# Layer 0's pairs in six tiles of 128 rows and one tile that holds the 34 left three times

## The reference

```python
e = stack([tbl_f[ids[:, f]] for f in range(39)], axis=1)        # (2048, 39, 16)
x0, xk = e, e
for idx, (W, b) in enumerate([(w0, b0), (w1, b1), (w2, b2)]):   # 128 outputs each
    z = relu(einsum('bhd,bkd,hks->bsd', x0, xk, W) + b)
    if idx != 2:
        xk = z[:, :64]
        direct.append(z[:, 64:])
    else:
        direct.append(z)
z = sum(concatenate(direct, axis=1), axis=-1)                   # (2048, 256)
h = concatenate([z, dense_ctx], axis=1)
h = relu(h @ W_top1 + b_top1); h = relu(h @ W_top2 + b_top2)
y = h @ W_top3
```

## Time and profile before

| | |
|---|---|
| time, median of 3 runs | 2412.33 us (2410.93 to 2412.48) |
| the profiled execution | 2410.21 us, span 2408.4 us |
| TensorE busy | 2343.9 us, 97% |
| VectorE busy | 2253.5 us, 94% |
| GpSimd busy | 2001.8 us, 83% |
| ScalarE busy | 1305.4 us, 54% |
| moved by DMA | 475.43 MB, mean 197 GB/s |
| granted TensorE clock, mean | 0.996 of full |

### The profile page before, as it was taken

The page is one execution under the profiler, slowest core; times in us unless marked ns, Lnnn a source line. Parts: engine busy times, 40 slices in busy tenths (PEclk is TensorE's granted clock), DMA queues, the critical chain, the costliest instruction groups (busy, mean ns, idle before and its releaser), DMA issues.

```text
span 2408.4 us, 32379 instructions
## 1 busy us (share of the span) xinstructions
PE 2343.9 (97%) x7936; PEld 1499.0 (62%) x7936; DVE 2253.5 (94%) x2241; ACT 1305.4 (54%) x1534; POOL 2001.8 (83%) x1284
## 2 busy tenths in 40 slices
PE   2899999999999999999999999999999999999999
PEld 1566666666666666666666666666666666666655
DVE  3799999999999999999999999999999999999973
ACT  2455555555555555555555555555555555555542
POOL 5888898898888889889888888988888888898630
PEclk9999999999999999999999999999999999999999
DMA  7977887787787788778778778877877887887610
GB/s 196 229 189 201 220 214 186 211 232 179 207 229 199 193 217 213 187 211 235 178 207 226 199 194 217 225 179 211 231 182 203 226 204 191 214 225 182 197 57 1
DMA packets 403715, 475.43 MB, mean 197 GB/s; under 512 B 171409, under 2 KB 180625, under 8 KB 403425
## 3 DMA queue, kind: packets, MB, share of 16 engines
q1 hardware_dynamic: 304055, 310.13, 52.8%
q10 hardware_dynamic: 79163, 159.95, 21.6%
q0 software_dynamic: 20480, 5.15, 1.8%
HBM read 465.41 MB, written 9.71 MB: 197 GB/s over the span
## 4 chain that ended last, share of the span: by engine, by line
PE 95%; POOL 2%; DMA 2%; issue 1%; SPq 0%; ACT 0%; DVE 0%; ACTq 0%; POOLq 0%
PE z L718 92%; POOL rows L515 1%; DMA xb<-x_rows 1%; POOL low L546 1%; DMA rows<-table,index 0%; PE x L813 0%; PE z L832 0%; PE prod_dve L813 0%; PE z L834 0%; PE z L791 0%; PE z L837 0%; SPq L426 0%; DMA x_rows<-rows 0%; PE x L814 0%; PE x L815 0%
## 5 line engine op out<-in xcount | busy, mean ns | idle before, releaser
L546 POOL TENSOR_TENSOR low<-prod_pool,high 128x1024 fp32r<-128x1024 f32 (+1 forms) x576 | 1379.4, 2395 | 206.8 <-ACT high L886 200.1
L718 PE MATMUL z<-prod_whole,w_whole 128*128 128x512 f32 (+2 forms) x2432 | 1130.5, 594 | 42.2 <-DVE prod_whole L601 42.2
L718 PE MATMUL z<-high,w_high 128*128 128x512 f32 (+1 forms) x1792 | 864.4, 482 | 17.9 <-ACT high L886 13.7
L886 ACT ACTIVATE high<-prod_pool 128x1024 fp32r<-128x1024 f32 (+1 forms) x576 | 611.0, 1061 | 407.5 <-DVE prod_pool L601 234.5
L718 PEld LDWEIGHTS z<-prod_whole,w_whole 128*128 128x128 f32 (+2 forms) x2432 | 461.8, 190 | 426.9 <-issue 365.6
L718 PE MATMUL z<-high,w_low 128*128 128x512 f32 (+1 forms) x1792 | 708.4, 395 | 0.0
L515 POOL DMA_INDIRECT rows<-table,index x640 | 611.1, 955 | 116.0 <-issue 102.2
L601 DVE TENSOR_TENSOR prod_pool<-xh,x 128x1024 f32<-128x1024 f32 x512 | 622.8, 1216 | 36.4 <-ACT x L864 33.3
L601 DVE TENSOR_TENSOR prod_whole<-xh,x 128x1024 f32<-128x1024 f32 (+1 forms) x576 | 615.6, 1096 | 6.1
L886 ACT ACTIVATE high<-prod_dve 128x1024 fp32r<-128x1024 f32 (+2 forms) x384 | 338.8, 882 | 481.6 <-DVE prod_dve L601 319.3
L718 PE MATMUL z<-low,w_high 128*128 128x512 f32 (+1 forms) x1664 | 554.4, 427 | 0.6 <-POOL low L546 0.6
(11 more groups left out here) (59 smaller groups left out, 405.2 us busy)
## 6 DMA issues: line engine op xcount, KB each, us to landing
xh<-x_rows SPq DMA_DIRECT2D x63, 2560.0 KB, 17.7
xh<-x_rows ACTq DMA_DIRECT2D x63, 2432.0 KB, 19.2
xb<-x_rows SPq DMA_DIRECT2D x128, 546.0 KB
xb<-x_rows SPq DMA_DIRECT2D x63, 468.0 KB
xa<-x_rows SPq DMA_DIRECT2D x191, 78.0 KB
rows<-table,index POOLq DMA_INDIRECT x640
xh<-x_rows SPq DMA_DIRECT2D x65, 128.0 KB, 20.5
x_rows<-rows SPq DMA_DIRECT2D x256, 20.0 KB
```

Of the source, the lines that this page charges most:

```text
L546: pool.tensor_tensor(low[0:g.rows, g.split_slot, 0:n, :], prod_pool[0:g.rows, g.slot, 0:n, :], high[0:g.rows, g.split_slot, 0:n, :].bitcas ...
L718: return pe.matmul(z[stage][:, :], weights[0:g.rows, table[stage, g.tiles[i]], :], src[0:g.rows, i, :], start=g.begins_layer and first, st ...
L886: act.activation(high[0:g.rows, g.split_slot, 0:n, :], src[0:g.rows, 0:n, :], ACT.Copy).then_inc(high_ready, 1)
```

## The change

Layer 0 gets six tiles of 128 rows: 117 as before (REST = 6 tiles of three shifts) and eleven rows of a further shift, 18 + tile (`MORE`, `MORE_AT`). Of the 780 pairs 34 are left. The seventh tile, number 6, holds 40 rows with these pairs three times, at rows 0, 40 and 80. VectorE multiplies it (from `xa_rest`), ScalarE rounds all of it, VectorE overwrites the first 40 rows with the low parts, and the weights are laid out so that rows 0 to 79 have w_high and rows 80 to 119 w_low. One rounded pass (`rest_pass`) then does what three do elsewhere. Tiles 0 and 1 become WHOLE, tile 6 BY_DVE; there is no BY_DVE pair in layer 0 any more.

The loads of pairs per chunk grow from six DMAs to twenty: two for the eleven rows (22 KB and 132 KB), and four for each copy of the 40 rows, each of ten outer rows by two, 40 KB. The rows of the low parts' copy are the first. The unused rows are cleared once. The MLP's second context input moves to a product slot, as there are 27 instead of 28 split weight tiles.

```diff
-T0 = -(-SHIFTS // JT)
-LAST0 = (SHIFTS - JT * (T0 - 1)) * F
+T0 = SHIFTS // JT + 1
+REST = T0 - 1
+MORE = 128 - JT * F
+MORE_AT = JT * REST
+LEFT, LEFT_AT, LEFT_RUN, LEFT_STEP = 40, 10, 10, 19
+FOR_HIGH_W, FOR_LOW_W = (0, LEFT), (2 * LEFT,)
...
-    0: [(WHOLE, 6, 1), (BY_DVE, 0, 2), (BY_POOL, 2, 2), (WHOLE, 4, 2)],
+    0: [(WHOLE, 0, 2), (BY_DVE, REST, 1), (BY_POOL, 2, 2), (WHOLE, 4, 2)],
...
+X0_LOADS = 2 * JT + 2 + 12
...
-                    "ctx": [w[0:CTX, CTX_AT:CTX_AT + MB], w[0:CTX, CTX_AT + MB:CTX_AT + 2 * MB]],
+                    "ctx": [w[0:CTX, CTX_AT:CTX_AT + MB], x[0:CTX, 4 + n1, :]],
...
-        def load_pairs(engine, c, shifts):
+        def load_pairs(engine, c, shifts, rest):
             of = rows_of(c)
+            step = of.ap[0][0]
             for jj in shifts:
-                n = (SHIFTS - jj + JT - 1) // JT
                 at = slice(jj * F, (jj + 1) * F)
                 engine.dma_start(xa[at, :], of[0:F, :]).then_inc(x0_loaded, 16)
-                step = of.ap[0][0]
                 shifted = bass.AP(tensor=of.tensor, offset=of.offset + jj * step,
-                                  ap=[[step, F], [JT * step, n], [1, CN]])
-                engine.dma_start(xb[at, 0:n, :], shifted).then_inc(x0_loaded, 16)
+                                  ap=[[step, F], [JT * step, REST], [1, CN]])
+                engine.dma_start(xb[at, 0:REST, :], shifted).then_inc(x0_loaded, 16)
+            if not rest:
+                return
+            engine.dma_start(xa[JT * F:128, :], of[0:MORE, :]).then_inc(x0_loaded, 16)
+            shifted = bass.AP(tensor=of.tensor, offset=of.offset + MORE_AT * step,
+                              ap=[[step, MORE], [step, REST], [1, CN]])
+            engine.dma_start(xb[JT * F:128, 0:REST, :], shifted).then_inc(x0_loaded, 16)
+            for at in FOR_HIGH_W + FOR_LOW_W:
+                for s in range(2):
+                    half = slice(at + s * LEFT // 2, at + (s + 1) * LEFT // 2)
+                    for rows, field in ((xa_rest, LEFT_AT + s), (xb[:, REST, :], LEFT_AT + LEFT_STEP)):
+                        runs = bass.AP(tensor=of.tensor, offset=of.offset + field * step,
+                                       ap=[[step, LEFT_RUN], [LEFT_STEP * step, 2], [1, CN]])
+                        engine.dma_start(rows[half, :], runs).then_inc(x0_loaded, 16)
...
+                else:
+                    sp.wait_ge(rest_cleared, 2)
-                load_pairs(sp, c, range(2 if c.known and c.n == 0 else JT))
+                load_pairs(sp, c, range(2 if c.known and c.n == 0 else JT), True)
...
-                part = slice(H, 128) if g.half else slice(0, g.rows)
-                into = (high if g.half else low)[part, g.split_slot, 0:n, :]
+                part = slice(H, 128) if g.half else slice(0, LEFT) if g.rest else slice(0, g.rows)
+                into = (high if g.stacked else low)[part, g.split_slot, 0:n, :]
...
+                    other = xa_rest if g.rest else shared
...
+            dve.memset(xa_rest[:, :], 0.0).then_inc(rest_cleared, 1)
+            dve.memset(xb[:, REST, :], 0.0).then_inc(rest_cleared, 1)
...
+                    if g.rest:
+                        dve.tensor_tensor(w_low[:, to, :], stage_sb[:, T0:T0 + 1, :],
+                                          w_low[:, to, :].bitcast(f32), ALU.subtract).then_inc(w_ready, 1)
+                        dve.wait_ge(w_ready, ready - 1)
+                        dve.tensor_tensor(w_high[:, to, :], w_high[:, to, :].bitcast(f32),
+                                          w_low[:, to, :].bitcast(f32), ALU.add).then_inc(w_ready, 1)
+                        continue
...
+                def rest_pass(g):
+                    wait_count(pe, low_by_dve, c, g, g.of_kind + 1, BY_DVE)
+                    mm(g, w_high, SPLIT_TILE, high[:, g.split_slot, :, :], 0, True, True
+                       ).then_inc(products_used, 1)
...
-                act.activation(xa_ps[0:JT * F, :], xa[:, :], ACT.Copy).then_inc(xa_copied, 1)
+                act.activation(xa_ps[:, :], xa[:, :], ACT.Copy).then_inc(xa_copied, 1)
...
-            load_pairs(act, Chunk(0, 0), range(2, JT))
+            load_pairs(act, Chunk(0, 0), range(2, JT), False)
```

More of the change, by code:

```diff
@@ L107, in __init__ @@
         self.half = stage > 0 and first == HALF_TILE
-        self.rows = 128 if stage else (LAST0 if first == T0 - 1 else JT * F)
+        self.rest = stage == 0 and first == REST
+        self.rows = 128
+        self.stacked = self.half or self.rest
         self.split = self.kind != WHOLE
@@ L131, in in_order_of_use @@
     for g in groups:
-        late = g.split and not g.half
-        if behind and (late or g.half or g.ends_layer):
+        late = g.split and not g.stacked
+        if behind and (late or g.stacked or g.ends_layer):
             yield behind
@@ L665, in _ @@
                     to, src = weight_tiles(g)
+                    dve.wait_ge(w_rounded, sum(1 + before.rest for before in firsts[:i + 1]))
+                    ready += 1 + g.half + g.rest
+                    if g.rest:
[5 more added lines that the diff above has]
+                        continue
                     part = slice(0, H) if g.half else slice(0, 128)
-                    dve.wait_ge(w_rounded, i + 1)
                     dve.tensor_tensor(w_low[part, to, :], src[part], w_high[part, to, :].bitcast(f32),
@@ L762, in contract @@
                         half_passes(g)
+                    elif g.rest:
+                        rest_pass(g)
                     elif g.ends_layer:
@@ L772, in chunk @@
                 contract(2, c)
-            pe.wait_ge(w_ready, sum(g.split for g in PLAN[0, 0]))
-            pe.wait_ge(w_rounded, len(GROUPS[0]))
+            pe.wait_ge(w_ready, sum(g.split + g.rest for g in PLAN[0, 0]))
+            pe.wait_ge(w_rounded, sum(1 + g.rest for g in PLAN[0, 0]))
             contract(0, Chunk(0, 0))
             pe.wait_ge(w_ready, W_READY)
-            pe.wait_ge(w_rounded, N_GROUPS)
+            pe.wait_ge(w_rounded, N_ROUNDED)
             over_chunks(pe, chunk)
@@ L1002, with place @@
     w0 = a["L0_rec_w0"]
-    w0a = np.zeros((128, T0, S), w0.dtype)
-    w0b = np.zeros((128, T0, S), w0.dtype)
-    first = np.arange(F)
-    for j in range(SHIFTS):
-        second = (first + j) % F
-        at = slice(j % JT * F, (j % JT + 1) * F)
-        w0a[at, j // JT] = w0[first, second]
-        if j:
-            w0b[at, j // JT] = w0[second, first]
+    w0a = np.zeros((128, STAGED0, S), w0.dtype)
+    w0b = np.zeros((128, STAGED0, S), w0.dtype)
+    placed = set()
+    def place(f, g, at, tile):
+        if f != g:
+            w0b[at, tile] = w0[g, f]
+        w0a[at, tile] = w0[f, g]
+        placed.add(frozenset((f, g)))
+    for tile in range(REST):
+        for jj in range(JT):
+            for f in range(F):
+                place(f, (f + JT * tile + jj) % F, jj * F + f, tile)
+    for tile in range(REST):
+        for f in range(MORE):
+            second = (f + MORE_AT + tile) % F
+            if frozenset((f, second)) not in placed:
+                place(f, second, JT * F + f, tile)
+    left = []
+    for r in range(LEFT):
+        s, k, run = np.unravel_index(r, (2, LEFT_RUN, 2))
+        f = int(LEFT_AT + s + LEFT_STEP * run + k)
+        pair = (f % F, int(LEFT_AT + LEFT_STEP * (run + 1) + k) % F)
+        if frozenset(pair) not in placed:
+            placed.add(frozenset(pair))
+            left.append((r, pair))
+    for tile, copies in ((REST, FOR_HIGH_W), (T0, FOR_LOW_W)):
+        for r, pair in left:
+            for at in copies:
+                place(*pair, at + r, tile)
+    assert len(placed) == F * (F + 1) // 2
     def by_fields(w):
```

39 lines of the change are left out of this document (23 added, 16 removed).

## The result

| | before | after |
|---|---|---|
| median | 2411.63 us (4 runs, 2410.14 to 2412.48) | 3018.15 us (4 runs, 3013.23 to 3022.27) |
| ratio | 1 | 1.252, interval 1.2503 to 1.2537 |
| a chunk, from the first last relu to the last one | 35.30 us | 44.56 us |

A forecast was written before the change was run, and what follows sets the result against it. TensorE's own pace was taken to bound the kernel after the start, at 35.37 us a chunk. 2410.2 - 18.6 + 7.5 = 2399.1, and 2.1 more for a median: 2401 us, range 2394 to 2410.

The forecast's parts named there:

- TensorE 0.30 us less a chunk: TensorE's layer 0: 5.36 us becomes 5.06 a chunk; over 62 chunks 18.6 us less.
- VectorE makes one single and three pair products as before: VectorE's layer 0: products unchanged, low part 0.53 us less, so about 34.3 of 35.07 us busy.
- 14 more issues, 0.5 us apart: SyncE's loads of pairs, twenty instead of six a chunk: 6.9 us more issuing, hidden by its other waits.
- the third rival: Pairs come too late in every chunk at ScalarE's copy of xa: slower, 2513 us with copies 0.8 us each; chance 0.15.
- 24 packets x 0.148 = 3.6 us: Steady-state pair loads: the added 0.49 MB, cut in ten outer rows on ten engines, lands 3.6 us later.
- up to 7: Steady-state pair loads: delay in us of the added bytes if they take turns with ScalarE's xh stream.
- I take 4: Steady-state pair loads: chosen delay 4 us, landing at about 1027 against a limit of about 1030.6; steady state pays nothing.
- xh comes 4 us later, 10 us before it is wanted: The xh load in the steady state: 4 us later behind the added pairs, still 10 us early.
- the second leg: From the copy of xa to the next first load of pairs; 15.8 us would have been left for it.
- Everything behind 74.8 moves by: Start: 3 us for chunk 0's loads plus 4.5 for chunk 1's pairs, together 7.5 us, bounds 3.6 and 11.7.
- the ring: Copy of xa, then VectorE's layer 0 and sums, which release the next stores and loads; bites beyond 7.8 us later landing.
- the first leg: From the first load of pairs to the copy of xa; the prediction allowed 19.6 us (1010.96 to 1030.6).

The follow-up runs named there:

- free copies: Changed kernel with the copies loaded in chunk 0 only and xa_rest copied to PSUM by ScalarE before VectorE multiplies: 2399.13 us.
- the kernel before with twelve loads: Kernel before, plus twelve 40 KB loads into a buffer nobody reads, which the copy of xa waits for: 2887.39 us.
- the run with twenty rows: Changed kernel, each load of copies taking twenty consecutive rows instead of ten rows by two (wrong pairs): 2798.79 us.

## Why the prediction was wrong

- *TensorE 0.30 us less a chunk*: right. 35.05 us with free copies.
- *VectorE makes one single and three pair products as before*: wrong for the single one, which took 0.68 us before. The nearest row had one factor in PSUM; here both are in SBUF, 1.1 us on average in the changed kernel and 2.06 where GpSimd is busy. With the copies loaded once the kernel took 2426.7 us with this product and 2399.1 with one factor in PSUM.
- *14 more issues, 0.5 us apart*: mis-sized. The twelve copies cost 0.88 each (10.6 us); more than the 0.8 of the third rival.
- *"24 packets x 0.148 = 3.6 us", "up to 7", "I take 4"*: this step failed, and it decides. Landing moved from the 11.8 us reckoned to over 24, not to 16. The pairs were through 12.5 us after their first issue, nearly as reckoned; the 240 rows of the copies took 12.2 us more, not 4. With ScalarE's xh kept away they took 5.4, so the 3.6 was not far off for a queue by itself. What was mis-sized is the term "taking turns with ScalarE's xh stream it is up to 7", which was priced by counting queues. That the copies suffer from this stream is shown by moving it (24.75 to 17.3 us). Why so much is argued only: the copies' last rows (80 to 119) and ScalarE's xh (64 to 127) lie in one half, and in 1024 to 1029 the two queues share 207 GB/s, of which the copies' queue gets 0.19 of 1.03 MB. That a shared half has this effect is shown for xh against xh alone, and few engines for a load stay a rival.
- *xh comes 4 us later, 10 us before it is wanted*: wrong in kind. Not only its start moved. The halves of xh fell out of step and ran at 207 to 209 GB/s for much of their time instead of 398, and 17.7 us to landing became 27.2. SyncE's half then lay in its queue before the stored rows, whose issue took 4.5 us in the mean instead of 3.0 (5.83 in the period shown): most of what the second leg grew by.
- *"Everything behind 74.8 moves by" 7.5 us*: mis-sized in both of its terms. Copies of `xa` for chunk 1, before, in the changed kernel and in the one with copies in chunk 0 alone and `xa_rest` in PSUM:

```profile
74.79 0.60 ACT L877 ACTIVATE xa_ps<-xa 117x512 f32<-117x512 f32 x1 [11.92 <-DMA xb<-x_rows]
```
```profile
95.57 0.60 ACT L933 ACTIVATE xa_ps<-xa 128x512 f32<-128x512 f32 x1 [23.00 <-DMA xb<-x_rows]
```
```profile
83.95 0.60 ACT L936 ACTIVATE xa_ps<-xa 128x512 f32<-128x512 f32 x1 [11.78 <-DMA xb<-x_rows]
```

  So 9.2 us for chunk 0's loads (I took 3; chunk 0's own copy of `xa` is at 50.55 us instead of 40.69), and 11.6 for chunk 1's copies (4.5). In the run with copies loaded once but without PSUM it was at 86.96, which makes 12.2 and 8.6; either way the sum is 20.8, not 7.5. That the run with PSUM came out at 2399.1, the number of my sum, is partly luck: it has 9.2 instead of 7.5 at the start without chunk 1's copies, against 0.32 instead of 0.30 in each chunk.
- *The third rival*: right in place (ScalarE's copy of `xa`) and in that the ring closes; that it bites at just 19.6 us no run isolates. Its price, 1.8 us a chunk, was 9.3, since it counted the issue alone and left the ring's other leg as it was.

No version here beats the kernel before with all of its output. Open: half of the 130 us between the kernel before with twelve loads and the changed one; why two loads into opposite halves can fall to 209 and 279 GB/s; and whether copies loaded by both queues into opposite halves would keep the first leg under 19.6 us and xh in step. That wasn't tried.

## What to carry to other kernels

Before a stream is added, write down for each queue which partitions it fills at what time: two streams into one half of the partitions shared half of the rate here (207 against 404 GB/s), and engines that are 80% or 100% busy don't tell. A load that delays its queue can put two later, well-matched streams out of step; look for pairs of transfers that run together and ask if they still will. When a new operand's price is taken from the nearest row, compare not only its size but where each operand lies.

## What was not expected of the hardware

- A DMA's issue on SyncE took 0.78 us, 0.88 apart, when source (ten rows by two) and destination (twenty rows) are cut differently, and 0.29, 0.38 apart, when alike (the run with twenty rows); the loads of pairs, alike on both sides too, took 0.3 to 0.36.
- The busy share of the DMA engines is no rate. With ScalarE's xh 6 us late nearly the same bytes move in 1000 to 1035.5 us, 203 GB/s instead of 205, at a share of 0.94 instead of 0.80. In the changed kernel the share is 1.07 both at 96 GB/s and at 209; the share says how long packets took, not what they moved.
- A VectorE product of 512 columns with both factors in SBUF took 2.08 us under a GpSimd instruction, three times its 0.69.
